# Attention scores of a two-part transformer layer on all eight 64 x 32 tiles of TensorE

## What is computed

```python
qkv = (x @ qkv_w.T).reshape(Bb, Nn, 3, H, hd).transpose(2, 0, 3, 1, 4)
q, k, v = (qkv[0], qkv[1], qkv[2])
attn = jnp.einsum('bhnd,bhmd->bhnm', q, k) * scale
m = _local_mask(WINDOW, Nn)          # (w - |i-j|/2)/w for i-8 <= j < i+8, else 0
attn = jnp.where(m != 0.0, attn * m, -jnp.inf)
attn = jax.nn.softmax(attn, axis=-1)
out = jnp.einsum('bhnm,bhmd->bhnd', attn, v)
```

## Time and profile before

| what | us |
|---|---|
| executions, all | 449.06, 456.13, 516.21 |
| their median | 456.13 |
| the profiled execution, its own time | 446.29 |
| its span in the profile | 444.4 |
| PE busy in the span | 384.4 (86%) |
| DVE busy in the span | 255.1 (57%) |

### The profile page before, as it was taken

The page is one execution under the profiler, slowest core; times in us unless marked ns, Lnnn a source line. Parts: engine busy times, 40 slices in busy tenths (PEclk is TensorE's granted clock), DMA queues, the critical chain, the costliest instruction groups (busy, mean ns, idle before and its releaser), DMA issues.

```text
span 444.4 us, 11754 instructions
## 1 busy us (share of the span) xinstructions
PE 384.4 (86%) x4806; PEld 277.6 (62%) x4806; DVE 255.1 (57%) x498; ACT 137.8 (31%) x293; POOL 137.8 (31%) x155
## 2 busy tenths in 40 slices
PE   3598989879899999978597993899999999989973
PEld 0456778667778787856453472677777777764451
DVE  0258687847687877999945786332222222311596
ACT  1311223313243433321134432233333333432420
POOL 6200204004030303030467870033334334341442
PEclk9698999969999999999769896999999999999988
DMA  8115581976935353425023262233333232105812
GB/s 291 32 53 131 154 177 54 209 275 164 219 95 157 96 159 99 131 86 124 1 74 105 95 201 71 61 106 108 96 103 107 92 106 64 55 1 158 268 52 90
DMA packets 53066, 52.44 MB, mean 118 GB/s; under 512 B 22148, under 2 KB 48045, under 8 KB 52406
## 3 DMA queue, kind: packets, MB, share of 16 engines
q1 hardware_dynamic: 40976, 28.81, 24.8%
q0 software_dynamic: 4528, 12.40, 9.2%
q10 hardware_dynamic: 7510, 10.49, 7.2%
HBM read 28.75 MB, written 20.79 MB: 111 GB/s over the span
## 4 chain that ended last, share of the span: by engine, by line
PE 67%; DVE 19%; issue 6%; DMA 3%; POOL 2%; ACT 1%; SPq 0%; ACTq 0%; DVEq 0%; POOLq 0%
PE bank L1345 13%; PE bank L1360 9%; PE bank L1286 9%; PE bank L1127 7%; PE bank L1187 5%; PE bank L1166 5%; PE bank L1296 3%; PE bank L1175 3%; DVE second_region L782 2%; PE bank L1329 2%; PE bank L1353 2%; DVE region L759 2%; DMA modb<-moddram 2%; PE bank L1103 2%; PE bank L1158 2%
## 5 line engine op out<-in xcount | busy, mean ns | idle before, releaser
L507 POOL DMA_INDIRECT yrows<-second_region,sloti x47 | 46.2, 984 | 88.5 <-ACT second_region L674 87.7
L1029 DVE COPY second_region<-bank 128x256 f32<-128x256 f32 x47 | 19.9, 424 | 83.3 <-PE bank L1329 83.3
L1345 PE MATMUL bank<-region,second_region 128*128 x188 | 64.2, 465 | 0.5 <-DVE second_region L1029 0.4
L1360 PE MATMUL bank<-w,second_region 88*128 x188 | 48.6, 380 | 1.1 <-ACT second_region L669 1.1
L452 POOL TENSOR_TENSOR rstd2s<-ve,cft 128x2 f32<-128x2 f32 x8 | 5.6, 706 | 134.7 <-DVE ve L807 134.7
L782 DVE RECIPROCAL second_region<-bank 128x256 f32<-128x256 f32 x16 | 28.1, 1757 | 29.9 <-PE bank L1193 29.8
L1286 PE MATMUL bank<-xT_region,sw 128*128 128x512 f32 (+1 forms) x96 | 45.2, 630 | 0.0
L1187 PE MATMUL bank<-region 128*32 128x16 f32 x2048 | 35.8, 215 | 8.7 <-issue 7.5
L1187 PEld LDWEIGHTS bank<-region 128*32 128x32 f32 x2048 | 34.0, 159 | 14.3 <-issue 12.9
L1345 PEld LDWEIGHTS bank<-region,second_region 128*128 128x128 f32 x188 | 32.0, 190 | 12.8 <-issue 2.5
L472 POOL DMA_INDIRECT hslots<-hx,posi x32 | 34.4, 1074 | 9.5 <-issue 9.5
(11 more groups left out here) (159 smaller groups left out, 612.1 us busy)
## 6 DMA issues: line engine op xcount, KB each, us to landing
second_region<-hslots SPq DMA_DIRECT2D x47, 128.0 KB, 2.0
hslots<-zeros ACTq DMA_DIRECT2D x5, 1024.0 KB, 8.2
region<-vd SPq DMA_DIRECT2D x32, 128.0 KB, 4.4
region<-yrows SPq DMA_DIRECT2D x16, 256.0 KB, 6.2
modb<-moddram SPq DMA_DIRECT2D x8, 384.0 KB, 4.1
w<-w2T POOLq DMA_DIRECT2D x4, 704.0 KB, 9.2
xs<-x SPq DMA_DIRECT2D x8, 256.0 KB, 8.0
region<-second_region SPq DMA_DIRECT2D x64, 32.0 KB, 2.3
```

The lines of the kernel that those rows point to most:

```text
L507: gp.indirect_dma_start(yrows, bass.IndirectOffsetOnAxis(ap=sloti[:, s:s + 1], axis=0), yo[:, s % RING, :], None, bounds_check=TOPK * T - ...
L1029: dve.tensor_copy(rT[:, s % 2].rearrange("p c t -> p (c t)"), RTP).then_inc(rT_s, 1)
L1345: last = pe.matmul(UP(s), rT[:, s % 2, c, :], w13[:, c, bass.ds(experts[s], 1), :], start=c == 0, stop=c == C - 1)
L1360: last = pe.matmul(YP(s), hT2[0:IH, s % 2, k, :], w2[:, k, bass.ds(experts[s], 1), :], start=k == 0, stop=k == 1)
```

## The change

Every octet now has its 64 features in both halves of the partitions. The upper 64 partitions hold the tokens of the first 64 of each half `u`, the lower 64 those of the last 64, so blocks 0 to 3 use rows 0 to 63 and blocks 4 to 7 rows 64 to 127, for all octets. `scores` runs once over four steps `k`, and each step uses all eight tiles (row half, column group). The mask is two full-array matmuls of 512 columns per call of `scores` in place of eight of 32 output columns. `product` makes q and k in that layout: for each octet, each of two feature groups and each partition half, one matmul of 64 output columns and 128 tokens. `kT` has 16 edge columns for each octet and half, so `keep_k` copies the bulk in one activation and the keys that a neighbouring half needs in four small ones that read one partition half and write the other. `qbd` is filled by the same 8 DMAs per batch with rows of 512 bytes in place of 1024. The clearing of `kT` on POOL covers 640 columns in place of 544.

```diff
--- before.py
+++ after.py
@@ -28,6 +28,7 @@
 G = D // OC
 BL = P // QB
 NBLK = G * GH
+HB = P // 2
 PADN = WIN + N + WIN
 EPS = 1e-5
 
@@ -145,9 +146,10 @@
         region = sb("region", [P, 12288])
         at = C * GH * N
 
-        qbd = region[:, 0:at].rearrange("p (c h n) -> p c h n", c=C, h=GH)
-        kT = attn.take("c n", (C, PADN,))
-        qT = attn.take("c n", (C, N,))
+
+        qbd = region[:, 0:at].rearrange("p (o h n) -> p o h n", o=G, h=GH)
+        kT = attn.take("o u n", (G, U, WIN + HB + WIN,))
+        qT = attn.take("o n", (G, U * HB,))
         vS = attn.take("u d", (U, D,))
 
 
@@ -415,7 +417,7 @@
         @block.gpsimd
         def _(gp):
             gp.memset(pb[:, :], 0.0).then_inc(pads, 1)
-            gp.memset(kT[:, :, :], 0.0).then_inc(pads, 1)
+            gp.memset(kT[:, :, :, :], 0.0).then_inc(pads, 1)
 
             gp.wait_ge(c_silu, 1)
             gp.memset(qbd, 0.0).then_inc(pads, 1)
@@ -559,14 +561,21 @@
             def keep_q(b):
                 wait(act, q_p, b + 1)
                 wait(act, q_e, 16 * GH * b)
-                act.activation(qT[:, :, :].rearrange("p c n -> p (c n)"), M1, ACT.Copy).then_inc(q_s, 1)
+                act.activation(qT[:, :, :].rearrange("p o n -> p (o n)"), M1, ACT.Copy).then_inc(q_s, 1)
 
             def keep_k(b):
                 wait(act, k_p, b + 1)
                 if b == 0:
                     act.wait_ge(pads, 2)
                 wait(act, s_p, U * b)
-                act.activation(kT[:, :, WIN:WIN + N], M0.rearrange("p (c n) -> p c n", c=C), ACT.Copy).then_inc(k_s, 1)
+                made = M0.rearrange("p (o u n) -> p o u n", o=G, u=U)
+                act.activation(kT[:, :, :, WIN:WIN + HB], made, ACT.Copy)
+
+                up, low = slice(0, HB), slice(HB, P)
+                act.activation(kT[up, :, :, WIN + HB:], made[low, :, :, 0:WIN], ACT.Copy)
+                act.activation(kT[low, :, :, 0:WIN], made[up, :, :, HB - WIN:], ACT.Copy)
+                act.activation(kT[up, :, 1, 0:WIN], made[low, :, 0, HB - WIN:], ACT.Copy)
+                act.activation(kT[low, :, 0, WIN + HB:], made[up, :, 1, 0:WIN], ACT.Copy).then_inc(k_s, 1)
 
             def keep_v(b):
                 wait(act, v_p, b + 1)
@@ -1120,12 +1129,15 @@
                                             xn[:, u, c * P:(c + 1) * P], ident)
                 last.then_inc(hT_p, 1)
 
-            def product(o, off, done):
-
-                for c in range(C):
+            def product(out, off, done):
+
+                for o in range(G):
                     for k in range(C):
-                        last = pe.matmul(o[:, c * N:(c + 1) * N], wqkv[:, k, off + c * P:off + (c + 1) * P],
-                                         hT[:, k, :], start=k == 0, stop=k == C - 1)
+                        for half in range(2):
+                            tokens = hT[:, k, :].rearrange("p (u y n) -> p u y n", u=U, y=2)[:, :, half, :]
+                            last = pe.matmul(out[HB * half:HB * (half + 1), o * P:(o + 1) * P],
+                                             wqkv[:, k, off + o * OC:off + (o + 1) * OC], tokens,
+                                             start=k == 0, stop=k == C - 1, skip_group_check=True)
                 last.then_inc(done, 1)
 
             def make_q(b):
@@ -1152,20 +1164,18 @@
                 wait(pe, k_s, it + 1)
                 wait(pe, ga_s, n - U + 1)
 
-                for turn in range(2):
+                for half in range(2):
+                    pe.matmul(SP[u][:, half * 512:(half + 1) * 512], identb,
+                              addmask[:, u, 2 * half:2 * half + 2].unsqueeze(2).to_broadcast([P, 2, GH, 2 * QB]),
+                              start=True, stop=False, skip_group_check=True)
+                for k in range(BL // 2):
                     for o in range(G):
-                        half = (o + turn) % 2
-                        pe.matmul(SP[u][KB * o:KB * (o + 1), half * 512:(half + 1) * 512], identb[:, KB * o:KB * (o + 1)],
-                                  addmask[:, u, 2 * half:2 * half + 2].unsqueeze(2).to_broadcast([P, 2, GH, 2 * QB]),
-                                  start=True, stop=False, skip_group_check=True)
-                    for k in range(BL // 2):
-                        for o in range(G):
-                            c, s = divmod(o, 2)
-                            b = k + BL // 2 * ((s + turn) % 2)
-                            q0 = u * P + b * QB
+                        for half in range(2):
+                            b = k + BL // 2 * half
+                            rows = slice(HB * half, HB * (half + 1))
                             last = pe.matmul(SPV[u][KB * o:KB * (o + 1), b // 2, :, b % 2, :],
-                                             kT[OC * s:OC * (s + 1), c, q0:q0 + KB],
-                                             qbd[OC * s:OC * (s + 1), c, :, q0:q0 + QB],
+                                             kT[rows, o, u, k * QB:k * QB + KB],
+                                             qbd[rows, o, :, u * HB + k * QB:u * HB + (k + 1) * QB],
                                              start=False, stop=True, skip_group_check=True)
                 last.then_inc(s_p, 1)
```

## The result

The changed kernel's median is 468.36 us (465.76 to 469.51, 4 runs) beside 454.25 of the kernel before on the same chip: ratio 1.038, 95% interval [1.029, 1.048]. In a second comparison it was 1.020 [1.009, 1.031]. The forecast was 447, so its sign was wrong. The profiled execution took 469.51 us against 446.29. Each ratio leaves out executions in a slower state (over 1.5% above the fastest of their kernel), so it is not the quotient of the medians.

What follows compares the result with a forecast made beforehand. PE was taken to bound batches 4 to 6, other batches mostly DMA or DVE. Gains of 0.9 (batch 1) and 4.8 (batches 4 to 6) less 0.5 for the clock made 5.2 us: 452.6 to 447, range 435 to 461.

Steps and rivals of the forecast that it cites:

- The scores: Attention scores on eight tiles: a call falls from 2.67 to 1.56 us, 1.10 less for each of 16 calls.
- rivals 2 and 3: 2: no more starts per time than now, 452 us, chance 0.10; 3: half-wide products run one after another, 464, 0.07.
- The products: Products of q and k, 8 instructions become 32: still 1.7 us each, plus 0.25 per batch for tiling changes.
- Batches 2 and 3, "nothing but a longer stall": Batches 2 and 3 wait for values from DMA, so no gain; the 1.82 us stall grows to some 3.2.
- the 0.5 us I took for the clock: Loss from a slower PE clock after the longer stall of batches 2 and 3: up to 1.5 us, 0.5 taken.
- Batches 4 to 6, -4.8: PE-bound attention batches get shorter by 1.20, 1.56 and 2.05 us, together 4.8.
- the 0.85 a batch that I took for the second call and the products: Batches 4 to 6: second scores call gives 1.10 us, products take back 0.25.
- the 2.3 us that I took for DVE's waits: Batches 4 to 6: DVE's waits for scores vanish, gaining 0.35, 0.71 and 1.20 us.
- Batch 1, -0.9: Batch 1 gains 0.9 us: second scores call 0.85, product takes back 0.15, against 1.1 until v has landed.
- `keep_k` and `spread_q`: Four more ACT copies, +0.8 us per batch, covered by 3.00 idle; query-spreading DMA issues take no longer.
- rival 4: Queries come late: `spread_q` issues take twice as long, 3.9 of 5.2 us gone, 451 us; chance 0.08.
- Rival 1: Every call of scores counts because value landings move forward with PE: 15.6 us gone, 437; chance 0.17 whole or mostly.

Runs made afterwards that it cites:

- e3: Kernel before with only the products of queries and keys split as the change writes them, 384 matmuls more; ratio 1.043 [1.032, 1.054].
- e9: Changed kernel with whole products as in the kernel before, ScalarE sorting the halves while copying out; ratio 1.001 [0.996, 1.006].
- e7: Changed kernel with all loads of the experts' weights moved to the last batch's pass; 453.1 us (442.0 to 456.0).
- e8: Kernel before with all loads of the experts' weights moved to the last batch's pass; 451.6 us (444.5 to 452.1).
- e4: Changed kernel with the w2 and w13 loads moved to batches 4 and 5; no median given, 8.0 us from its pair at batch 7.
- e5: Kernel before with the w2 and w13 loads moved to batches 4 and 5; 452.6 us.
- e1: Changed kernel again, nothing edited, for a second profile; batch 7 at 208.1 us, whole time below the expected 465 to 470.
- e2: Changed kernel with queries laid out head, octet, token, so spreading writes 2 KB pieces instead of 512 bytes; 457.9 to 469.4 us.
- e13: Changed kernel with whole products and all loads of the experts' weights in the last batch's pass; 445.6 beside 460.0 us, ratio 0.981 [0.960, 1.002].
- e6: Kernel before again, nothing edited, for a second profile; batch 7 at 192.0 us, no own median given.

## Why the prediction was wrong

1. *The scores.* Right: 1.61 us a call against 1.56 forecast, so 1.06 less a call where 1.10 was forecast. 64 instructions in 1.16 us are 14 ns each with the last one's length taken off; the Trainium skill's 25 ns from start to start ("TensorE: Matmul & The Clock Gate", the section that the prediction names) does not hold for tiled matmuls. Row halves overlap, so rivals 2 and 3 were wrong in all their parts.
2. *The products.* The step that failed. I priced "8 instructions of 256 columns become 32" by PE's time, 1.7 to 2.0 us, plus 0.25 for changes of tiling. That was right for the time (1.97 us) and left out that instructions must be brought in: a term put at nothing. e3 has this step alone and loses what the change loses; e9 has everything but this step and loses nothing. Its price is 9 to 12 us (batch 7 at 205.6 and 208.1 with it, 196.2 without). The stops are shown, at the same count each time; their sum is not the whole price, since e9 is 8.4 us dry against 11.0 and 17.9. The rest is the clock behind the stops and the waits for the values (item 3). Without the loads the changed kernel is still 8.6 us behind at batch 7 (e7 beside e8), though the medians, 453.1 and 451.6, hardly show it. The Trainium skill, "Runtime: NRT & Kernel Launch", section "Instruction fetch mechanics", has the blocks of 256 instructions, which the trace confirms, and says that a crossing is mostly hidden; here 8 and 9 of the 30 crossings in the attention were not, at 11.0 and 17.9 us.
3. *Batches 2 and 3, "nothing but a longer stall".* The cause of the stall was right (e4, e5), the size not: the lag grows by 14.2 us there in the first profile. 13.21 - 5.13 = 8.1 are the wait for the values of batch 2, which I had said could only grow by what PE gains; they landed in `vbd` 25.5 us after they had been written to memory, before 18.8, though issued at the same times (76.5 to 78.0 and 76.3 to 77.8 us). In e1, e2 and e3 it was 19.5, 20.5 and 17.9, in e4 25.0 (batch 5) against e5's 18.6. So more than half of what batches 2 and 3 lost in this profile hangs on a landing that varies from run to run; why it does stays open, and whether the change has a part in it. The rest is dry time (6.8 us there against 1.3) and the clock behind it: `turn_p` took 1.97 us at 103.75, as the earlier trace rows had 1.87, but the 0.5 us I took for the clock stands against a stretch of 34 us at 0.80.
4. *Batches 4 to 6, -4.8.* 2.9 us came out in the first profile, about 0.96 each, much as e13's 0.94 a batch. Six tenths of the size, and not sure: in e1 the same batches lost 2.1 us, with 6.0 us dry in them against 2.1. Where it came out it is close to the 0.85 a batch that I took for the second call and the products (3 x 0.85 = 2.55), and the 2.3 us that I took for DVE's waits (0.35, 0.71, 1.20) mostly did not come. No run shows what took their place. *Batch 1, -0.9.* The recorded sum has a slip, since the terms named there make 0.85 - 0.15 = 0.70. And 0.7 were lost: PE comes to `scores(1, 1)` ahead of DVE's residual and waits for it, then stops 1.5 us inside that call.

```profile
56.87 0.59 PE L1168 MATMUL bank<-cbt 128*128 128x512 bf16 x2 [1.22 <-DVE second_region L800]
```

5. *`keep_k` and `spread_q`.* Right: the four small activations take 0.82 us in batch 5 and 2.13 us idle are left behind them; the queries' eight issues took 6.75 us there and had landed by about 182, ahead of `scores(6, 0)` at 183.5. So rival 4 fell too.
6. *Rival 1*, that every call counts, fell with batches 2 and 3. No rival had the mechanism that decided. What should have shown it stood in the groups by line of before, beside the page's 39 fetches: the scores, which wait for nothing once begun, idle for "issue".

```profile
L1166 PE MATMUL bank<-region,second_region 64*32 64x128 f32 x1024 | 35.1, 272 | 1.0 <-issue 1.0
```

7. *Behind the attention.* Of the 23.3 us between the two profiled spans, 11.8 lie ahead of the last count. The 11.5 behind it vary by as much between two profiles of one kernel (13.3 us between before and e6), so they are no evidence against the change.

## What to carry to other kernels

Count the instructions of TensorE per microsecond as well as its busy time. Cutting a matmul into four on parts of the array can leave its time unchanged and still cost, if the stream around it is dense and DMA is busy; keeping the matmuls whole and paying for the layout in another engine's idle time (e9) took the whole loss away here. A step cut in two by idle time with "issue" behind it, inside a call with no wait, is the sign to look for.

## What the runs showed of the hardware

- TensorE's instructions come in fetches of 16 KB, 256 at a time. In 16 profiles it never started more than 449 instructions beyond 256 for each landed fetch, and where it had to wait it went on 1.2 to 1.7 us after a landing. The fetch's transfer takes 0.9 to 1.8 us; what varies is when it starts. In e7 one started at 130.8 us, 11 us behind the one ahead, 1.6 us after the last of the 2048 packets of 256 bytes of the values. That data transfers hold it up is what the timing suggests; I did not take the fetch's competitors away one by one.
- Fetches start as late in before. In its batches 2 and 3 two started 9.1 and 7.0 us after its instructions in hand had fallen to 256, while PE waited for the values, and 73 and 93 were left by then. In the changed kernel two started 9.1 and 7.4 us after that point, with 17 and 0 left; in e3 10.6 and 9.4, with none left. So late fetches are found in both kernels, and what differs is how much is in hand when they come.
- Before itself stops 3 to 6 times in the attention, 3 to 4 us in all, and where PE stood longest the granted clock was lower too: 0.88 in its batch 2, 0.77 in the changed kernel's.
- After the last count VectorE is released up to 7.2 us behind the matmuls' ends: at once in the first profile of before, after 1.95 us in e6, 7.17 and 6.51 in the two of the changed kernel (there ScalarE goes on 0.2 us behind VectorE). The stretch from the count to L1304 has 31 to 48 us, in kernels of either kind, and makes most of the scatter. Its cause stays open.
